# An attention kernel's order rewritten from steps of two key tiles to steps of one

## What is computed

```python
tp = silu(time_emb) @ Wt + bt            # shifts, scales, gates
h = layernorm(x, g1, be1) * (1 + scale_msa) + shift_msa
q, k, v = split(h @ Wqkv + bqkv)         # 16 heads of 32
attn = softmax(einsum('blhd,bmhd->bhlm', q, k) * HD ** -0.5)
out = einsum('bhlm,bmhd->blhd', attn, v)
x = x + gate_msa * (out @ Wproj + bproj)
h = layernorm(x, g2, be2) * (1 + scale_mlp) + shift_mlp
x = x + gate_mlp * (gelu(h @ W1 + b1) @ W2 + b2)
out = rmsnorm(x) * rms_weight * (1 + scale) + shift
```

## Time and profile before

| | before |
|---|---|
| median of three runs | 4077.82 us |
| profiled execution, its own time | 4073.34 us |
| its span | 4071.6 us |
| TensorE matmul busy | 3995.4 us, 98% |
| VectorE / ScalarE / GpSimd busy | 61% / 44% / 47% |
| one unit, from one transpose of the maxima (L535) to the next | 30.09 us with a projection, 27.98 us without |
| matmuls of the full array in a unit | 76 with a projection, 64 without |
| calls of values and denominators in a unit | 8 and 3, in seven blocks |

### The profile page before, as it was taken

The page is one execution under the profiler, slowest core; times in us unless marked ns, Lnnn a source line. Parts: engine busy times, 40 slices in busy tenths (PEclk is TensorE's granted clock), DMA queues, the critical chain, the costliest instruction groups (busy, mean ns, idle before and its releaser), DMA issues.

```text
span 4071.6 us, 51447 instructions
## 1 busy us (share of the span) xinstructions
PE 3995.4 (98%) x19723; PEld 2648.5 (65%) x19723; DVE 2473.4 (61%) x4020; ACT 1795.4 (44%) x3220; POOL 1923.4 (47%) x530
## 2 busy tenths in 40 slices
PE   8999999999999999999999999799999999999998
PEld 6778875445455455454455544588888888888886
DVE  3665557887777777777777775234445443344442
ACT  2222224665565555655555556333333333333332
POOL 1000005888788787887887878632211122231111
PEclk9999999999999999999999999999999999999999
DMA  5444463233323323323323330411110111201110
GB/s 199 175 173 176 183 210 102 53 73 76 75 64 82 78 53 84 76 55 84 74 65 74 74 78 26 142 55 42 34 42 34 42 39 50 62 34 42 34 42 21
DMA packets 184993, 323.70 MB, mean 80 GB/s; under 512 B 14452, under 2 KB 53428, under 8 KB 184748
## 3 DMA queue, kind: packets, MB, share of 16 engines
q1 hardware_dynamic: 184748, 320.41, 27.7%
HBM read 201.77 MB, written 117.54 MB: 78 GB/s over the span
## 4 chain that ended last, share of the span: by engine, by line
PE 94%; DVE 1%; DMA 1%; issue 1%; POOL 1%; ACT 1%; SPq 0%; POOLq 0%; ACTq 0%; DVEq 0%
PE psum L527 13%; PE psum L989 13%; PE psum L1002 12%; PE psum L428 10%; PE psum L430 9%; PE psum L429 9%; PE psum L1510 6%; PE psum L1514 6%; PE psum L1512 6%; PE psum L1018 4%; PE psum L1029 1%; PE psum L1031 1%; PE psum L1033 1%; PE psum L1472 1%; PE psum L463 1%
## 5 line engine op out<-in xcount | busy, mean ns | idle before, releaser
L817 DVE TENSOR_REDUCE max_part<-psum 128x1 f32<-128x512 f32 x2048 | 1298.6, 683 | 351.6 <-PE psum L527 340.8
L1121 ACT ACTIVATE probs<-psum 128x512 f32<-128x512 f32 x2048 | 1071.6, 599 | 686.1 <-PE psum L989 683.8
L1241 POOL TENSOR_TENSOR prob_sum<-prob_sum,probs 128x2048 f32<-128x2048 f32 x256 | 1175.8, 4593 | 111.7 <-ACT probs L1121 92.5
L1643 DVE TENSOR_TENSOR g_parts<-g_full,g_parts 128x512 fp32r<-128x512 f32 x256 | 311.7, 1217 | 776.0 <-ACT g_parts L1552 776.0
L527 PE MATMUL psum<-k_stack,q_stack 96*128 96x512 f32 x2048 | 758.2, 419 | 3.0 <-DVE max_part L817 1.3
L989 PE MATMUL psum<-q_stack,k_stack 98*128 98x512 f32 x2048 | 675.7, 411 | 4.9 <-DMA q_stack<-negmax_lo 2.5
L527 PEld LDWEIGHTS psum<-k_stack,q_stack 96*128 96x128 f32 x2048 | 387.5, 189 | 295.2 <-DVE max_part L817 235.9
L989 PEld LDWEIGHTS psum<-q_stack,k_stack 98*128 98x128 f32 x2048 | 372.1, 189 | 290.9 <-ACT probs L1121 250.2
L1548 ACT ACTIVATE g_full<-psum,cols 128x512 f32<-128x512 f32 x256 | 176.5, 690 | 823.4 <-PE psum L430 823.0
L1710 POOL TENSOR_TENSOR y_out<-y_out,rows 128x512 f32<-128x512 f32 x64 | 82.4, 1289 | 947.4 <-DVE y_out L1681 947.4
L1002 PE MATMUL psum<-probs,v_group 128*32 128x512 f32 x4096 | 517.4, 600 | 0.9 <-ACT probs L1121 0.9
(11 more groups left out here) (152 smaller groups left out, 4731.7 us busy)
## 6 DMA issues: line engine op xcount, KB each, us to landing
qk_parts<-qk_out SPq DMA_DIRECT2D x128, 512.0 KB, 2.8
k_stack<-qk_parts SPq DMA_DIRECT2D x96, 512.0 KB, 7.0
q_stack<-qk_parts SPq DMA_DIRECT2D x192, 256.0 KB, 9.4
x_in<-in_x SPq DMA_DIRECT2D x16, 1024.0 KB, 5.4
v_rows<-v_out SPq DMA_DIRECT2D x64, 256.0 KB, 2.0
v_group<-v_rows SPq DMA_DIRECT2D x32, 512.0 KB, 12.1
gated_attention<-gated SPq DMA_DIRECT2D x64, 256.0 KB, 4.6
x<-in_x SPq DMA_DIRECT2D x16, 1024.0 KB, 7.9
```

The source lines that it names most:

```text
L817: dve.reduce_max(max_part[:, n:n + 1], psum[:, SMAX[at.turn % 3], :], AX.X).then_inc(dve_smax, 1)
L1121: act.activation(probs[slot(u, s)][:, h, j, :], psum[:, ST[k % 3], :], ACT.Exp, scale=SCALE).then_inc(act_exp, 1)
L1241: pool.tensor_tensor(prob_sum[u % 2][:, :, :], prob_sum[u % 2][:, :, :], probs[slot(u, s)][:, :, j, :], ALU.add).then_inc(pool_sum, 1)
```

## The change

`ORDER` is rewritten in eight steps of one key tile. Maxima and scores alternate one by one. In a step stand four of each; the other work has letters of its own: V values of the tile before, D one call of the denominators, J a third of a projection (four matmuls), `!` the send; on VectorE g gate, t turn, r reciprocal, p spread, n normalise; on ScalarE w (weigh, L1093 before) and a (the projection's high part). `probs` becomes six buffers of one key tile; the bytes are the same. GpSimd still makes five additions a unit and its subtraction for the projection. The send stands in the fifth of eight steps instead of in the fourth of four, and 16 maxima instead of 9 are made ahead, so stage 1 makes 7 more. The tail starts with two thirds of a projection, and two projections stand ahead of the last denominators instead of one.

```diff
-    ORDER = (("mssm*mssm", "mssmm*mssmm"), ("mssm*mssm", "mssm*ssm"),
-             ("mssm*ssm", "mssm*ssm"), ("mssm*!mssm", "mssmm*mssm"))
-    LEAD = sum(x.count("m") for x in ORDER[-1])
+    ORDER = ("msmsJmsmsJV", "mswmsgmsmsV", "msmsDmsmsV", "msamsDmsmsV",
+             "msmsD!msmsV", "msmstmsmsrV", "msmspmsmsV", "nmsmsmsmsJV")
+    SUMMED = KT - 2
+    AHEAD = 2
+    LEAD = N_MAX + AHEAD - "".join(ORDER).split("!")[0].count("m")
+    PV_LAG = 1
+    RING = 6
...
-        probs = [s2(f"probs{i}", [P, GH, 2, CH]) for i in range(3)]
+        probs = [s2(f"probs{i}", [P, GH, CH]) for i in range(RING)]
...
         def pe_attention(pe, at):
+                for kt in range(KT):
+                    h = 0
+                    for what in ORDER[kt]:
+                        if what == "s":
+                            pe_score(pe, u, kt, h)
+                            h += 1
+                        elif what == "m":
+                            pe_maximum(pe, at)
+                        elif what == "!" and u + 1 < NU:
+                            pe_send_max(pe, at, u + 1)
+                        elif what == "V":
+                            if kt >= PV_LAG:
+                                pe_values(pe, u, kt - PV_LAG)
+                            elif u:
+                                pe_values(pe, u - 1, kt - PV_LAG + KT)
+                        elif what == "D" and u:
+                            pe_denominators(pe, u - 1, dens)
+                            dens += 1
+                        elif what == "J" and kt == 0:
+                            if u - PROJ_LAG >= 1:
+                                pe_project_part(pe, u - PROJ_LAG - 1, DEN_BANK, parts)
+                            parts += 1
+                        elif what == "J" and u - PROJ_LAG >= 0:
+                            pe.wait_ge(dve_attn, u)
+                            pe_project_part(pe, u - PROJ_LAG, DEN_BANK, 0)
...
         def pe_tail(pe):
             at = TAIL[0]
-            pe_values(pe, NU - 1, LAST, 0)
-            pe_values(pe, NU - 1, LAST, 1)
-            pe.wait_ge(dve_gated, at)
+            pe_project_part(pe, at - 1, DEN_BANK, 1)
+            pe_project_part(pe, at - 1, DEN_BANK, 2)
+            pe_values(pe, NU - 1, LAST)
+            pe.wait_ge(dve_smax, FIRST_TAIL)
+            pe_project(pe, at, tail_bank(at))
             pe_denominators(pe, NU - 1, 0)
             pe_denominators(pe, NU - 1, 1)
-            pe.wait_ge(dve_smax, FIRST_TAIL)
-            pe_project(pe, at, tail_bank(at))
+            pe_project(pe, at + 1, tail_bank(at + 1))
             pe_denominators(pe, NU - 1, 2)
```

More of the change, by code:

```diff
@@ L1037, in pe_step_work, with pe_project_part @@
[L1037 to L1056 removed]
+        def pe_project_part(pe, n, bank, part):
+            hi, lo = attn_hi[n % 2], attn_lo[n % 2]
+            if part == 0:
+                pe.wait_ge(act_ahi, n + 1)
+                pe.wait_ge(pool_alo, n + 1)
+                if n == 0:
+                    pe.wait_ge(dve_wprojlo, 1)
+            for m in range(part * KD, (part + 1) * KD):
+                k, kind = divmod(m, 3)
+                left, right = ((hi, wproj_hi), (hi, wproj_lo), (lo, wproj_hi))[kind]
+                i = pe.matmul(psum[:, bank, :], left[:, k, :], right[:, k, :], start=m == 0,
+                              stop=m == 3 * KD - 1)
+            if part == 2:
+                i.then_inc(pe_proj2, 1)
@@ L1058, in pe_attention @@
+        def pe_project(pe, n, bank):
+            for part in range(3):
+                pe_project_part(pe, n, bank, part)
         def pe_attention(pe, at):
@@ new lines, in act_attention @@
+                for kt in range(KT):
+                    k = u * KT + kt
+                    if k >= RING:
+                        pu, pk = divmod(k - RING, KT)
+                        act.wait_ge(pe_pv, k - RING + 1)
+                        if pk >= SUMMED:
+                            act.wait_ge(pe_den, 3 * pu + pk - SUMMED + 1)
+                        else:
+                            act.wait_ge(pool_sum, sums_done(pu, pk))
+                    h = 0
+                    for what in ORDER[kt]:
+                        if what == "s":
+                            n = k * GH + h
+                            act.wait_ge(pe_st, n + 1)
+                            act.activation(probs[slot(u, kt)][:, h, :], psum[:, ST[n % 3], :],
+                                           ACT.Exp, scale=SCALE).then_inc(act_exp, 1)
+                            h += 1
+                        elif what == "w" and u:
+                            act_weigh(act, u - 1)
+                        elif what == "a" and tile >= 0:
+                            act_project(act, tile)
@@ L1380, in dve_tail @@
             dve.wait_ge(pe_den, 3 * NU)
[L1381 to L1382 removed]
+            dve.wait_ge(pool_sum, sums_done(NU - 1, SUMMED - 1))
+            for n, tile in enumerate(TAIL[2:], 2):
                 dve_gate(dve, tile, tail_bank(tile))
```

203 lines of the change are left out of this document (58 added, 145 removed).

## The result

The changed kernel takes **4150.26 us** (median of 4 runs, 4149.51 to 4157.24) against 4077.83 us before (4077.25 to 4080.38): ratio 1.018, 95% interval 1.0163 to 1.0198. It is 72 us slower; forecast were 86. The profiled execution of after took 4157.24 us, 7 above its median, that of before ran 4.5 under its own, so the two traces lie 84 us apart where the medians lie 72 apart. Two executions of kernels further down took 4950.64 and 4366.35 us at a mean granted clock of 0.75 and 0.85 instead of 0.99, and are left out of every comparison.

What follows compares the result with a forecast made beforehand. TensorE, busy 98% of the span, was taken as the bound. Units 9 to 61 add 74.7 us, units 1 to 8 6.1, unit 62 0.84, the tail 4: 4077.8 + 85.6 = 4163 us, range 4114 to 4192.

Steps and rivals of the forecast that it cites:

- More blocks: TensorE, each unit: 11 single blocks replace 4 double and 3 single; four splits at 0.35 each, +1.40 us a unit.
- Old waits go: TensorE's waits for PSUM banks, put down to paired maxima, all vanish: -0.56 us a unit, -1.21 without a projection.
- A new wait on VectorE: Steps 6 to 8: the 12th maximum waits for the ninth's bank, 0.46 plus 0.11: +0.57 us a unit, bounds 0 to 1.0.
- small operations in a row: VectorE, steps 6 to 8: turn 0.62, reciprocal 0.16, spread 0.63 and normalisation 0.59 us, together 2.00.
- t, r, p and n add up from step 6 on: VectorE's queue from step 6: these four total 2.00 us; under 1.54 VectorE would keep up without the new wait.
- rival A: VectorE keeps up: all terms as forecast but for the 0.57 us wait; 4129 us, chance 0.22.
- What stays covered: GpSimd, ScalarE, buffers and loads inside a unit stay hidden; 0.1 us if the cover of w goes.
- 7 maxima more in stage 1: Stage 1 makes 7 more maxima, unit 62 makes 7 fewer: net nothing.
- The tail: End of the attention: two denominator calls and a projection more ahead of the last denominators, +4.9 counted, +4 taken, bounds 0 to 6.
- The sum: Whole kernel: units 9 to 61 74.7, units 1 to 8 6.1, unit 62 0.84, tail 4: +85.6 us, 4163 us.
- Rival B: Waits on top: ScalarE's wait returns at each of 11 blocks and V waits for w, +27 us, 4190 us; chance 0.08.
- Rival C: Faster: the 0.10 and 0.11 surcharges beside a block are bank waits that alternating removes; -50 us, 4028 us, chance 0.07.

Runs made afterwards that it cites:

- run 1: Kernel before with each of its four double blocks cut in two, one maximum and one score between the halves: 4161.74 us against 4075.52, ratio 1.0209.
- first run of part 4: Changed kernel with the first two calls of denominators moved next to values, nine blocks a unit instead of eleven: 4110.70 us against before's 4075.52, ratio 1.0084.
- run 2: Kernel before with maxima and scores alternating one by one instead of in pairs, blocks kept: 4085.85 us against 4075.52, ratio 1.0026.
- part 5: Changed kernel with the last unit's denominators back in before's order, ahead of the projection that waits for GpSimd: 4147.94 us against before's 4075.53, ratio 1.0177.
- split: Kernel before with its four double blocks each cut into two single ones, eleven blocks a unit, before's tail: 4161.74 us against 4075.52, ratio 1.0209.
- alternate: Kernel before with maxima and scores one by one inside each half step, before's blocks and tail: 4085.85 us against 4075.52, ratio 1.0026.
- n_later: Changed kernel with VectorE's normalisation moved behind the first maximum of step 8: executions 4126.28, 4127.06 and 4130.98 us against before's 4076.19, ratio 1.0126.

## Why the prediction was right, and where it was not

Direction and range hold (4150 in 4114 to 4192), and so do the two terms that decide. Step by step, per unit with a projection:

- **More blocks, +1.40.** Right: 0.34 for each split (run 1) and 0.33 for each merged (first run of part 4), about 1.34 in all. The full matmul's pace, 0.2335 instead of 0.23, is the same in both kernels and cancels.
- **Old waits go, -0.56.** The size is right: of the measured 1.24 the splits are 1.34 and the new wait 0.45, which leaves -0.55 for the old ones. The reason isn't borne out. It was put down to pairs of maxima, and alternating alone left the sum of the waits as it was (run 2). So the right size is in part luck, since what does remove the waits is not shown. Without a projection it is about as right: the unit grew by 0.56, and moving n took 0.38 off it, so 0.56 - 1.34 - 0.38 leaves -1.16, forecast were -1.21.
- **A new wait on VectorE, +0.57.** Right in place and shape, a tenth too long. Counted from step 6's first matmul (1555.29), the ninth maximum starts at 7.23 (forecast 7.34) and the twelfth's load is released at 7.96 (8.07); TensorE would have been there at 7.60 (1562.66 + 0.23). Wait 0.36, and 0.11 behind it: 0.47 in this unit, and **0.45** in the mean of 20, as the run with n moved has it too. The term for the small operations in a row was 0.1 too high. The step that failed is the statement that t, r, p and n add up from step 6 on and decide together against 1.54: the queue all but runs empty at step 7, and moving t changed 0.04. The way to rival A led over n's place, not over the sum.
- **What stays covered.** Right: in a unit GpSimd is 24.19 of 31.34 busy and ScalarE 18.06, the values start 0.32 to 0.34 behind the matmul ahead of them, and no stall names GpSimd or a DMA. "7 maxima more in stage 1: nothing": +1.8 there (from the first send to the first score 19.1 us instead of 17.3) and 7 x 0.23 = 1.6 less at the end, also right.
- **The tail, +4 (0 to 6).** Close: 5.3 to 5.8 at a like clock (part 5), where 4.9 were counted and 4 taken. Against the one trace of before it looks like 8.5 and 7.1, since that trace has no fall of the clock in its tail; `split` and `alternate`, with the same tail, take 2.7 and 1.8 us longer there. The prediction has no term for the clock.
- **The sum.** Attention +67.0 in place of 81.6: 53 x 0.17 + 8 x 0.20 = 11 of these 15 us are the units, the largest part of it the 0.12 of the VectorE wait, and the rest lies at the attention's two ends. The tail, clock included, gives 4.5 back, so 85.6 - 14.6 + 4.5 = 75.5 from there on, and stage 1's 7.0 of this execution, most of them its own, make the 82.3 between the spans (less 0.2 in the MLP). In the second trace of the changed kernel, 75.5 above before's (4148.88 - 4073.34), the same stretches are 2.2, 66.4 and 7.1. The first score stood at 646.6 to 653.7 us over the executions of these kernels, so a few us of any such difference are stage 1's.

Rival A was a kernel that can be made: `n_later` is its unit (30.87, forecast 30.93), and its ratio of 1.0126 makes 4129 us of before's 4077.83. Rival B fell: no ScalarE wait returned at the blocks. Rival C fell with run 1. The rule of the Trainium skill behind it ("TensorE: Matmul & The Clock Gate", Part 3, "The mechanism") is narrower than the prediction gives it: a weight load is pulled ahead when it targets a row group that doesn't conflict, or the background weight buffer. The trace agrees between full matmuls, where the load starts 0.23 us ahead of its matmul; behind a block it doesn't start ahead.

Open is why a block costs a third of a microsecond beside its matmuls. The runs vary how many there are, and not what changes at their edges: the number of columns and the two passes of full float32 operands change together, and no run separates them. Another bank isn't enough: inside a block the step from denominators to values changes the bank and costs nothing (1.85 us for the two calls, as for two calls of values), and maxima and scores change it with each matmul. Why the loads at a block's two edges don't start ahead is as open. For the tail, what decides in which execution the clock falls isn't shown.

## What to carry over

Where TensorE is the bound, count how often the stream goes from full-array matmuls to column work and back, and price it from starts in the timeline (here 0.34 us a time, so four more in each of 62 units are 84 us): the same 19723 matmuls took 4162 us with eleven such blocks a unit and 4034 us with six, and 5 x 0.336 x 62 = 104 of these 128 us are the blocks. Pieces of under a microsecond were a cost of their own here, not a way to hide one. With a helper engine that frees a small ring of banks, look where in its queue each long operation stands: the same work cost 0.45 us a unit less with one operation behind the maximum whose bank is needed next instead of ahead of it, and about 0.4 less with the normalisation out of the step that carries the send, where turn and spread had moved too.

## What the hardware showed that was not expected

- The price of a block was the same with two full matmuls between two blocks as with eight: 1.00 to the next start, 0.33 ahead, 0.33 to 0.34 behind. Further calls in the same block cost 0.87 and then 0.85.
- Behind a matmul that stalled 0.36 us for a bank, the next start is 0.34 us away instead of 0.23, though its own bank is free. A stall thus costs 0.11 more than it lasts. The kernel before shows the same behind each of its 20 stalls of 0.14 to 0.16 us (20 units), and not behind most that last under 0.05.
- In the same place, an idle stretch of 4.15 us was followed by a projection that ran 4.8 us at a granted clock of 0.50, and one of 2.47 us by 3.4 us at that clock, while after 2.51 and 3.34 us it stayed at 1.00. The length of the idle stretch alone doesn't tell.
